# Cross attention's scores: the product of high queries with low keys on half of the array's rows, two query tiles side by side

## The chip, the cores and the metric

The kernel runs on one core of a Trainium2 chip. The metric is the device time of one execution in microseconds. The core's engines work side by side, each with its own queue, and meet by semaphores: TensorE (PE in the rows; PEld is its loading of weights), VectorE (DVE), ScalarE (ACT), GpSimd (POOL), and SyncE (SP), which here issues the loads and stores.

## The reference, cut to what matters

One decoder block over 4 batches of 512 rows by 512 columns, in float32: self attention with 16 heads, cross attention with 8 heads of 64 without projections, and a feed-forward with ternary weights, each behind a layer norm and added to its input. The change is in cross attention:

```
qh = q.reshape(B, h, dq, Lq);  kh = k.reshape(B, h, dq, Lk);  vh = v.reshape(B, h, dv, Lk)
scale = 1.0 / jnp.sqrt(jnp.asarray(dq, dtype=q.dtype))
qk = jnp.einsum('bhdq,bhdl->bhql', qh, kh) * scale
sm = jax.nn.softmax(qk, axis=-1)
ret = jnp.einsum('bhql,bhdl->bhdq', sm, vh)
...
x = x + _L0_xattn_ref(_layernorm(x, axis=-1), ctx_2048, ctx_2048, L0_xattn_gamma)
```

Here B = 4, h = 8, dq = dv = 64 and Lq = Lk = 512: a head's scores are a 512x512 matrix with a contraction over 64.

## The kernel before

Two parts follow each other on the one core. Self attention runs first, in two passes of two batches. Then comes the part that the change touches, in five turns (`turns`): turn 0 is cross attention of batch 0 alone; turns 1, 2 and 3 are cross attention of batch b with the feed-forward of batch b-1 woven between; the last turn is the feed-forward of batch 3 alone. Turns 1 and 2 are two rounds of one loop. In the trace, turn 0 begins at 812 us, turn 1 at 901, turn 2 at 1015, turn 3 at 1133.

Products are made in a reduced float32 format (`F32R`). So that they come out precise, an operand is split in a high part, a rounded copy, and a low part, which is what the copy lost. A query head has only 64 rows, so the array's 128 rows hold both parts at once: `qst` has the query's high part on rows 0 to 63 and its low part on rows 64 to 127, and `kh` and `kl` hold the key's high and low part on both halves. One product of 128 rows by 512 columns with `kh` gives (high + low query) x high key, a second one with `kl` adds (high + low query) x low key. Two products per tile of 128 queries make the scores in one bank of PSUM (lines 394 and 395, in `pe_sx`).

A turn walks 8 heads, and a head 4 query tiles; such a step is called a slot here. In a slot of head h and tile q every engine does its piece, in an order that is written out by hand:

- TensorE (`pe_turn`): scores of tile q (`pe_sx`); in slot 0 four transposes for the values (`pe_vt`, L372); four transposes of the probabilities of tile q of the head before (`pe_pt`, L384); in slots 1 and 3 half of an earlier head's output (`pe_ret`, L406 and L407, 8 products of 256 columns); and, in 22 of the 32 slots of turns 1 to 3, one piece of the feed-forward (`pe_up`, L420 and L421, 8 products of 512 columns).
- VectorE (`dve_turn`): the maximum of the score tile (L595), the low part of the values (slot 0, L584), the feed-forward's elementwise work, the low part of the probabilities (L590), the reciprocal, and in slot 0 the next head's queries (`dve_q`, L578).
- ScalarE (`act_turn`): the feed-forward's tanh (L519), the high part of the values (slot 0, L500) and of the probabilities (L505), the exponential of the score tile with its row sum (L509, two instructions: the activation and the read-out of the sum), in slot 0 the preparation of the next head's high parts (`act_prep`, L493 for `kh`, L495 for `qst`), and the high part of the feed-forward's gate (L526).
- POOL (`pool_turn`): normalising the probabilities (L744), the low parts of the next head (`pool_prep`, L734 for `kl`, L738 for `qst`), the low part of the gate (L751).

The score tiles alternate between two banks: tile q goes to bank q mod 2. So the scores of tile q wait until the exponential of tile q-2 has read its bank (`s_free`, in `pe_sx`); the first tile of a head also waits for POOL's low parts (`ql`, `kl`). SyncE loads a head's queries and keys two heads ahead, when POOL and TensorE have read the slot.

Of the kernel before, what the change touches and what calls it, by code (L numbers as in the profile page):

```python
# [16 lines left out]
F32 = mybir.dt.float32  # L17
F32R = mybir.dt.float32r
I32 = mybir.dt.int32
ACT = mybir.ActivationFunctionType  # L20
ALU = mybir.AluOpType
AX = mybir.AxisListType.X

P = 128
B, T, C = 4, 512, 512
# [8 lines left out]
XH, XD = 8, 64  # L34
# [44 lines left out]
def decoder_block(nc, x, ctx, wa, wb, wq_t, bq_col, bkv, bo, gamma, w1t, w3t, w2t, out):  # L79
# [8 lines left out]
    with stack:  # L88
# [3 lines left out]
        s = {}  # L92
# [138 lines left out]
        def sb(name, shape, dt=F32):  # L231
            return mem_b.enter_context(nc.sbuf_tensor(name, shape, dt))
# [10 lines left out]
        x1d = sb("x1d", [P, 2, C])  # L243
        kd = sb("kd", [P, 2, C])
        qst = sb("qst", [P, 2, C], F32R)
        kh, kl = sb("kh", [P, 2, C], F32R), sb("kl", [P, 2, C], F32R)
        vts = sb("vts", [P, 4, CK, P], F32R)
        pe_x = sb("pe_x", [P, 4, C])
# [7 lines left out]
        s_bank, t_bank, r_bank, u_bank = bank[0:2], bank[2:4], bank[4], bank[5:7]  # L256
        y_bank = [bank[7], bank[5]]

        S_TILES = 4 * XH
# [14 lines left out]
        def pieces(n):  # L274

            if n < 0 or n >= S_TILES:
                return range(0)
            return range(U_PIECES * n // S_TILES, U_PIECES * (n + 1) // S_TILES)
# [88 lines left out]
        def pe_vt(pe, b, h):  # L367
            pe.wait_ge(s[f"kd_in{h % 2}"], b * 128 + 32 * (h // 2 + 1))
            pe_wait(pe, "t_free", t_v(b, h), 2)
            tb = t_bank[(5 * h - 4 if h else 0) % 2]  # L370
            for c in range(CK):
                mm = pe.transpose(tb[:, c * P:(c + 1) * P], kd[:, h % 2, c * P:(c + 1) * P], ident[:])  # L372
            mm.then_inc(s["t_ready"], 1)

        def pe_wait(pe, free, index, ring):
            if not isinstance(index, int) or index >= ring:
                pe.wait_ge(s[free], index - (ring - 1))

        def pe_pt(pe, b, h, q):
            pe.wait_ge(s["xpn"], b * S_TILES + (4 * h + q + 1))  # L380
            pe_wait(pe, "t_free", t_p(b, h, q), 2)
            tb = t_bank[t_p(0, h, q) % 2]
            for c in range(CK):
                mm = pe.transpose(tb[:, c * P:(c + 1) * P], pe_x[:, q, c * P:(c + 1) * P], ident[:])  # L384
            mm.then_inc(s["t_ready"], 1)

        def pe_sx(pe, b, h, q):
            if q == 0:
                pe.wait_ge(s["ql"], b * XH + (h + 1))
                pe.wait_ge(s["kl"], b * XH + (h + 1))  # L390
            pe_wait(pe, "s_free", b * S_TILES + (4 * h + q), 2)
            lhs = qst[:, h % 2, q * P:(q + 1) * P]

            pe.matmul(s_bank[q % 2][:], lhs, kh[:, h % 2, :], start=True, stop=False)  # L394
            pe.matmul(s_bank[q % 2][:], lhs, kl[:, h % 2, :], start=False, stop=True).then_inc(s["s_ready"], 1)  # L395

        def pe_ret(pe, b, h, half):

            n = b * XH + h
            pe.wait_ge(s["t_free"], t_p(b, h, 2 * half + 1) + 1)  # L400
            if half == 0:
                pe_wait(pe, "r_free", n, 1)
            cols = slice(2 * P * half, 2 * P * (half + 1))
            for c in range(CK):
                lhs = vts[:, h % 4, c, :]
                pe.matmul(r_bank[:, cols], lhs, pxh[:, c, cols], start=c == 0, stop=False)  # L406
                mm = pe.matmul(r_bank[:, cols], lhs, pxl[:, c, cols], start=False, stop=c == CK - 1)  # L407
            mm.then_inc(s["r_ready"], 1)

        def pe_up(pe, f, piece):  # L410
            i, w = piece // 2, piece % 2
            m = chunk_rows(i)
            if piece == 0:
                pe.wait_ge(s["w_in"], 64)
                pe.wait_ge(s["t_free"], t_x3(f, TJ))
                pe.wait_ge(s["y"], 1 + f * TJ)
            pe.wait_ge(s[f"u{w}_free"], 1 + f * HC + i)
            for c in range(CK):
                lhs = w13[:, w, c, i * P:i * P + m]
                pe.matmul(u_bank[w][0:m, :], lhs, x3h[:, c, :], start=c == 0, stop=False)  # L420
                mm = pe.matmul(u_bank[w][0:m, :], lhs, x3l[:, c, :], start=False, stop=c == CK - 1)  # L421
            mm.then_inc(s[f"u{w}_ready"], 1)

        def pe_down(pe, f, t):
            pe.wait_ge(s["gl2"], 1 + f * HC + HC)
            if t >= 2:
                pe.wait_ge(s["y"], 1 + f * TJ + (t - 1))
            if t == 1:
                pe.wait_ge(s["u0_free"], 1 + f * HC + HC)
            for i in range(HC):  # L430
                k = chunk_rows(i)
                pe.matmul(y_bank[t % 2][:], gth[0:k, i, t * P:(t + 1) * P], w2[0:k, i, :], start=i == 0, stop=False)  # L432
                mm = pe.matmul(y_bank[t % 2][:], gtl[0:k, i, t * P:(t + 1) * P], w2[0:k, i, :], start=False, stop=i == HC - 1)  # L433
            mm.then_inc(s["y_ready"], 1)

        def pe_x3(pe, b, t):
            pe.wait_ge(s["x3n"], b * TJ + (t + 1))
            pe_wait(pe, "t_free", t_x3(b, t), 2)
            tb = t_bank[t_x3(0, t) % 2]
            for c in range(CK):  # L440
                mm = pe.transpose(tb[:, c * P:(c + 1) * P], pe_x[:, t, c * P:(c + 1) * P], ident[:])
            mm.then_inc(s["t_ready"], 1)

        def pe_turn(pe, b, f, nxt):
            for h in range(XH):
                for q in range(4):
                    if b is not None:
                        pe_sx(pe, b, h, q)
                        if q == 0:
                            pe_vt(pe, b, h)  # L450
                        if h:
                            pe_pt(pe, b, h - 1, q)
                        if q == 1 and h >= 2:
                            pe_ret(pe, b, h - 2, 1)
                        if q == 3 and h >= 1:
                            pe_ret(pe, b, h - 1, 0)
                    if f is not None:
                        for piece in pieces(4 * h + q):
                            pe_up(pe, f, piece)
            if b is not None:  # L460
                pe_pt(pe, b, XH - 1, 0)
                pe_ret(pe, b, XH - 2, 1)
                pe_pt(pe, b, XH - 1, 1)
                pe_pt(pe, b, XH - 1, 2)
            if f is not None:
                pe_down(pe, f, 0)
            if b is not None:
                pe_pt(pe, b, XH - 1, 3)
                pe_ret(pe, b, XH - 1, 0)
                pe_ret(pe, b, XH - 1, 1)  # L470
            if f is not None:
                for t in range(1, TJ - 1):
                    pe_down(pe, f, t)
            if b is not None:
                pe_x3(pe, b, 0)
                pe_x3(pe, b, 1)
            if f is not None:
                pe_down(pe, f, TJ - 1)
            if b is not None:
                for t in range(2, TJ):  # L480
                    pe_x3(pe, b, t)

        def stage_b_pe(pe):
            turns(pe.Fori, lambda b, f, nxt: pe_turn(pe, b, f, nxt))


        def act_prep(act, b, h):

            n, slot = b * XH + h, h % 2
            act.wait_ge(s[f"kd_in{slot}"], b * 128 + 32 * (h // 2 + 1))  # L490
            if h >= 2 or not isinstance(b, int) or b > 0:
                act.wait_ge(s["s_ready"], b * S_TILES + 4 * (h - 1))
            act.activation(kh[:, slot, :], kd[:, slot, :], ACT.Copy).then_inc(s["kh"], 1)  # L493
            act.wait_ge(s["xq"], n + 1)
            act.activation(qst[:, slot, :], x1d[:, slot, :], ACT.Copy).then_inc(s["qh"], 1)  # L495

        def act_vt(act, b, h):
            tb = t_bank[(5 * h - 4 if h else 0) % 2][:].rearrange("p (c n) -> p c n", n=P)
# [232 lines left out]
        def pool_prep(pool, b, h):  # L731
            n, slot = b * XH + h, h % 2
            pool.wait_ge(s["kh"], n + 1)
            pool.tensor_tensor(kl[:, slot, :], kd[:, slot, :], kh[:, slot, :].bitcast(F32), ALU.subtract).then_inc(s["kl"], 1)  # L734
            pool.wait_ge(s["qh"], n + 1)

            pool.wait_ge(s["kl"], n + 1)
            pool.tensor_tensor(qst[XD:P, slot, :], x1d[XD:P, slot, :], qst[XD:P, slot, :].bitcast(F32), ALU.subtract).then_inc(s["ql"], 1)  # L738
            pool.wait_ge(s["ql"], n + 1)

        def pool_prob(pool, b, h, q):
# [776 lines left out]
```

## Time and profile before

| | |
|---|---|
| time, median of 3 runs | 1315.93 us (1315.62 to 1319.83) |
| the profiled execution, first to last instruction | 1316.8 us |
| TensorE busy | 1175.0 us, 89% |
| VectorE busy | 817.9 us, 62% |
| POOL busy | 620.2 us, 47% |
| ScalarE busy | 570.6 us, 43% |
| mean granted TensorE clock | 0.968 |

The profiled execution's own time is its span of 1316.8 us. Busy time is what an engine spends in instructions; consecutive instructions of one engine overlap, so the distance between two starts tells more of the rate than a duration does. In the timelines a row is: start in us from the span's start, duration in us, engine, line, operation, what is written and read, its shape, how many were merged in the row, and in brackets the idle time of the engine before it and what ended it.

### The profile page before, as it was taken

What the parts mean: (1) busy time and instruction counts of PE and PEld (TensorE: products, weight loads), DVE (VectorE), ACT (ScalarE), POOL (GpSimd) and SP (SyncE); (2) the same over time, 40 slices, a digit from 0 to 9 for tenths busy, and PEclk for the clock granted to TensorE, in tenths of its full rate; (3) what the DMA queues carried; (4) which work ended last, traced back from release to release, by engine and by line L of the source; (5) the groups of instructions that cost most, each with busy time, mean ns of one, the idle gap of its engine ahead of it and who ended that gap; (6) DMA issues with size and microseconds to landing.
All of it is one profiled execution on the core that took longest, in us unless ns stands there. A gap on an engine that the chain in (4) does not pass through costs nothing.

```text
span 1316.8 us, 18217 instructions
## 1 busy us (share of the span) xinstructions
PE 1175.0 (89%) x5728; PEld 955.6 (73%) x5728; DVE 817.9 (62%) x1430; ACT 570.6 (43%) x1193; POOL 620.2 (47%) x516
## 2 busy tenths in 40 slices
PE   3859989999995799988999997777999999999998
PEld 2648867777774578876777785566887787888786
DVE  8645665433448576666564657887885787688531
ACT  5323343424335224343323322766762874577130
POOL 3156764535433336764525442654651664365031
PEclk9889999999998799999999998998999999999999
DMA  6232242044152024242425413382111211210000
GB/s 223 73 128 80 80 142 73 26 127 135 40 168 80 0 78 139 80 137 80 150 93 172 135 64 112 97 302 72 47 47 44 85 32 40 89 49 17 33 1 32
DMA packets 52594, 118.56 MB, mean 90 GB/s; under 512 B 11413, under 2 KB 11413, under 8 KB 50482
## 3 DMA queue, kind: packets, MB, share of 16 engines
q1 hardware_dynamic: 52530, 117.79, 27.6%
q8 instruction: 30, 0.49, 0.2%
q14 instruction: 34, 0.28, 0.1%
HBM read 100.96 MB, written 16.81 MB: 89 GB/s over the span
## 4 chain that ended last, share of the span: by engine, by line
PE 49%; DVE 18%; issue 12%; POOL 10%; ACT 7%; DMA 3%; SPq 0%; POOLq 0%; DVEq 0%; ACTq 0%
POOL work L1438 7%; PE bank L74 7%; PE bank L76 6%; PE bank L75 6%; PE bank L421 6%; PE bank L420 6%; DVE raw_a L1257 5%; PE bank L384 4%; PE bank L432 3%; PE bank L433 3%; POOL wal L1432 3%; PE bank L394 2%; PE bank L395 2%; PE bank L406 2%; PE bank L407 2%
## 5 line engine op out<-in xcount | busy, mean ns | idle before, releaser
L1438 POOL TENSOR_TENSOR work<-tmp,work 128x512 fp32r<-128x512 f32 x120 | 154.2, 1295 | 247.8 <-ACT work L1134 163.6
L744 POOL TENSOR_SCALAR pe_x<-pe_x,xri,gam 128x512 f32<-128x512 f32 x128 | 101.0, 790 | 107.0 <-DVE xri L599 101.2
L420 PE MATMUL bank<-x3h,w 128*128 128x512 f32 (+1 forms) x352 | 141.4, 402 | 1.6 <-DVE x3l L664 1.6
L421 PE MATMUL bank<-x3l,w 128*128 128x512 f32 (+1 forms) x352 | 139.1, 395 | 0.0
L1432 POOL TENSOR_TENSOR wbl<-raw_b,wbh 128x512 fp32r<-128x512 f32 x64 | 91.2, 1459 | 64.1 <-ACT wbh L1082 64.1
L74 PE MATMUL bank<-wah,xth 128*128 128x512 f32 x256 | 101.7, 397 | 15.4 <-POOL wal L1432 15.4
L1432 POOL TENSOR_TENSOR wal<-raw_a,wah 128x512 fp32r<-128x512 f32 x64 | 92.3, 1472 | 47.6 <-ACT wah L1089 47.6
L74 PE MATMUL bank<-wbh,gh 128*128 128x512 f32 x256 | 103.1, 403 | 13.0 <-DVEq L1306 11.7
L74 PE MATMUL bank<-wbh,work 128*128 128x512 f32 x256 | 102.3, 399 | 6.9 <-DVE work L1323 4.9
L509 ACT ACTIVATE pe_x<-bank,xmx 128x512 f32<-128x512 f32 x128 | 87.8, 686 | 40.6 <-DVE xmx L595 39.3
L595 DVE TENSOR_REDUCE xmx<-bank 128x1 f32<-128x512 f32 x128 | 87.4, 683 | 27.3 <-PE bank L395 24.1
L1323 DVE TENSOR_TENSOR work<-bank,work 128x512 fp32r<-128x512 f32 x64 | 44.2, 691 | 96.6 <-ACT work L1140 96.3
L1317 DVE TENSOR_TENSOR tmp<-bank,bkv_bc 128x512 f32<-128x512 f32 x64 | 44.2, 691 | 92.8 <-PE bank L76 47.5
L76 PE MATMUL bank<-wbh,gl 128*128 128x512 f32 x256 | 101.8, 398 | 0.0
L75 PE MATMUL bank<-wbl,gh 128*128 128x512 f32 x256 | 101.8, 398 | 0.0
L75 PE MATMUL bank<-wal,xth 128*128 128x512 f32 x256 | 100.8, 394 | 0.0
L76 PE MATMUL bank<-wah,xtl 128*128 128x512 f32 x256 | 100.8, 394 | 0.0
L76 PE MATMUL bank<-wbh,work 128*128 128x512 f32 x256 | 100.0, 391 | 0.0
L1134 ACT ACTIVATE work<-tmp 128x512 fp32r<-128x512 f32 x64 | 40.4, 631 | 137.4 <-DVE tmp L1317 137.4
L75 PE MATMUL bank<-wbl,work 128*128 128x512 f32 x256 | 99.9, 390 | 0.0
L590 DVE TENSOR_TENSOR pxl<-bank,pxh 128x512 fp32r<-128x512 f32 x128 | 87.5, 686 | 14.4 <-ACT pxh L505 13.7
L1276 DVE SCALAR_TENSOR_TENSOR tmp<-bkv_bc,shat,bank 128x512 f32<-128x512 f32 x64 | 47.8, 746 | 78.0 <-POOL work L1438 44.3
(158 smaller groups left out, 3063.6 us busy)
## 6 DMA issues: line engine op xcount, KB each, us to landing
raw_b<-in_wb SPq DMA_DIRECT2D x16, 1024.0 KB, 5.6
raw_a<-in_wa SPq DMA_DIRECT2D x16, 1024.0 KB, 5.4
x1d<-x_scratch SPq DMA_DIRECT2D x64, 128.0 KB, 2.7
kd<-in_ctx SPq DMA_DIRECT2D x64, 128.0 KB, 2.7
ternary_scratch<-wraw SPq DMA_DIRECT2D x12, 682.5 KB, 5.6
wraw<-in_w1t SPq DMA_DIRECT2D x8, 682.5 KB, 4.9
wraw<-in_w3t SPq DMA_DIRECT2D x8, 682.5 KB, 7.2
wraw<-in_w2t SPq DMA_DIRECT2D x8, 682.5 KB, 9.5
```

Source lines behind the costliest of these rows:

```text
L74: pe.matmul(out, wh, xh, start=start, stop=False)
L75: pe.matmul(out, wh, xl, start=False, stop=False)
L76: return pe.matmul(out, wl, xh, start=False, stop=stop)
L420: pe.matmul(u_bank[w][0:m, :], lhs, x3h[:, c, :], start=c == 0, stop=False)
L421: mm = pe.matmul(u_bank[w][0:m, :], lhs, x3l[:, c, :], start=False, stop=c == CK - 1)
L509: act.activation(pe_x[:, q, :], s_bank[q % 2][:], ACT.Exp, bias=xmx[:, q:q + 1], accum_out=xrs[:, q:q + 1]).then_inc(s["s_free"], 1)
L590: dve.tensor_tensor(pxl[:, :, q * P:(q + 1) * P], tb, pxh[:, :, q * P:(q + 1) * P].bitcast(F32), ALU.subtract).then_inc(s["t_free"], 1)
L595: dve.reduce_max(xmx[:, q:q + 1], s_bank[q % 2][:], axis=AX, negate=True).then_inc(s["xmx"], 1)
L744: pool.tensor_scalar(pe_x[:, q, :], pe_x[:, q, :], xri[:, q:q + 1], gam[:], ALU.mult, ALU.mult).then_inc(s["xpn"], 1)
L1257: dve.tensor_tensor(raw_a[:, c, :], raw_a[:, c, :], beta_bc[:], ALU.add).then_inc(s["beta_add"], 1)
L1432: pool.tensor_tensor(low[:, c, :], raw[:, c, :], high[:, c, :].bitcast(F32), ALU.subtract).then_inc(s[f"w{which}l"], 1)
L1438: pool.tensor_tensor(low, tmp[:, slot, :], high.bitcast(F32), ALU.subtract).then_inc(s["mvl"], 1)
```

## The change

Per pair of query tiles the two products with `kh` stay as they are. The two products with `kl` are cut to the high query: for the first tile they use rows 0 to 63 of `qst` and `kl`, for the second rows 64 to 127 of a new tile `qsd`, which holds the high query on its upper half, and of `kl`. The two halves of the array work on different tiles and banks. What is left out is low query x low key.

- TensorE: `pe_sx` is called for q = 0 and 2 only, and makes the scores of q and q + 1: wait for bank q, product with `kh`; wait for bank q + 1, product with `kh`; then the two half products, each of which reports its tile as ready.
- ScalarE: the copy of `qst` covers rows 0 to 63; a second copy writes the high query to rows 64 to 127 of `qsd`. Each counts up `qh`.
- POOL: waits for two counts of `qh` per head, and takes the low query on rows 64 to 127 from `qsd` instead of from the same rows of `qst`.

```diff
+        qsd = sb("qsd", [P, 2, C], F32R)
...
         def pe_sx(pe, b, h, q):
             if q == 0:
                 pe.wait_ge(s["ql"], b * XH + (h + 1))
                 pe.wait_ge(s["kl"], b * XH + (h + 1))
-            pe_wait(pe, "s_free", b * S_TILES + (4 * h + q), 2)
-            lhs = qst[:, h % 2, q * P:(q + 1) * P]
-
-            pe.matmul(s_bank[q % 2][:], lhs, kh[:, h % 2, :], start=True, stop=False)
-            pe.matmul(s_bank[q % 2][:], lhs, kl[:, h % 2, :], start=False, stop=True).then_inc(s["s_ready"], 1)
+            for r in (q, q + 1):
+                pe_wait(pe, "s_free", b * S_TILES + (4 * h + r), 2)
+                pe.matmul(s_bank[r % 2][:], qst[:, h % 2, r * P:(r + 1) * P], kh[:, h % 2, :], start=True, stop=False)
+            for r, of, part in ((q, qst, slice(0, XD)), (q + 1, qsd, slice(XD, P))):
+                pe.matmul(s_bank[r % 2][:], of[part, h % 2, r * P:(r + 1) * P], kl[part, h % 2, :], start=False, stop=True).then_inc(s["s_ready"], 1)
...
-                        pe_sx(pe, b, h, q)
+                        if q % 2 == 0:
+                            pe_sx(pe, b, h, q)
...
-            act.activation(qst[:, slot, :], x1d[:, slot, :], ACT.Copy).then_inc(s["qh"], 1)
+            act.activation(qst[0:XD, slot, :], x1d[0:XD, slot, :], ACT.Copy).then_inc(s["qh"], 1)
+            act.activation(qsd[XD:P, slot, :], x1d[XD:P, slot, :], ACT.Copy).then_inc(s["qh"], 1)
...
-            pool.wait_ge(s["qh"], n + 1)
+            pool.wait_ge(s["qh"], n * 2 + 2)
...
-            pool.tensor_tensor(qst[XD:P, slot, :], x1d[XD:P, slot, :], qst[XD:P, slot, :].bitcast(F32), ALU.subtract).then_inc(s["ql"], 1)
+            pool.tensor_tensor(qst[XD:P, slot, :], x1d[XD:P, slot, :], qsd[XD:P, slot, :].bitcast(F32), ALU.subtract).then_inc(s["ql"], 1)
```

## Rows read from the trace of the kernel before

**Rows 1.** Busy time by stretch: length, then per engine, clock, DMA share, GB/s.
```profile
847.60:865.02 17.42, 13.92 (x88) 10.85 (x89) 15.66 (x34) 13.01 (x31) 11.41 (x12) 1.00 0.42 130
1036.03:1092.47 56.44, 56.38 (x333) 47.94 (x332) 47.84 (x96) 40.86 (x89) 36.71 (x37) 1.00 0.17 47
```
**Rows 2.** Groups by line: busy us, mean ns, idle before them and its releasers.
```profile
L394 PE MATMUL bank<-kh,qst 128*128 128x512 f32 x128 | 56.3, 440 | 15.6 <-ACT pe_x L509 15.5
L495 ACT ACTIVATE qst<-x1d 128x512 fp32r<-128x512 f32 x32 | 20.1, 630 | 10.2 <-DVE x1d L578 9.2
```
**Rows 3.** Timeline of TensorE, turn 2, head 6.
```profile
1080.92 0.40 PE L394 MATMUL bank<-kh,qst 128*128 128x512 f32 x1
1081.16 0.40 PE L395 MATMUL bank<-kl,qst 128*128 128x512 f32 x1
1081.39 0.60 PE L372 MATMUL bank<-ident,kd 128*128 128x128 f32 x4
1081.83 0.60 PE L384 MATMUL bank<-ident,pe_x 128*128 128x128 f32 x4
...
1085.99 0.40 PE L394 MATMUL bank<-kh,qst 128*128 128x512 f32 x1
...
1086.81 0.48 PE L420 MATMUL bank<-x3h,w 128*128 128x512 f32 x1
1087.13 0.40 PE L421 MATMUL bank<-x3l,w 128*128 128x512 f32 x1
...
1088.76 0.40 PE L394 MATMUL bank<-kh,qst 128*128 128x512 f32 x1
```
**Rows 4.** Timeline of ScalarE in that head, and busy time of its last stretch.
```profile
1084.68 0.63 ACT L495 ACTIVATE qst<-x1d 128x512 fp32r<-128x512 f32 x1 [0.42 <-DVE x1d L578]
1085.22 0.61 ACT L526 ACTIVATE gth<-gf 128x512 fp32r<-128x512 f32 x1
...
1087.35 0.21 ACT L509 ACTIVATION_READ_ACCUMULATOR pe_x<-bank,xmx 128x1 f32 x1
...
1084.68:1087.56 2.88, 2.88 (x22) 2.65 (x21) 2.28 (x4) 2.88 (x7) 2.73 (x3) 1.00 0.20 3
```
**Rows 5.** Timelines, turn 2, heads 2 to 4: tile 2's scores, exp(1)'s read-out.
```profile
1041.07 0.40 PE L394 MATMUL bank<-kh,qst 128*128 128x512 f32 x1
1041.39 0.20 ACT L509 ACTIVATION_READ_ACCUMULATOR pe_x<-bank,xmx 128x1 f32 x1
...
1052.87 0.39 PE L394 MATMUL bank<-kh,qst 128*128 128x512 f32 x1
1053.42 0.20 ACT L509 ACTIVATION_READ_ACCUMULATOR pe_x<-bank,xmx 128x1 f32 x1
...
1064.64 0.40 PE L394 MATMUL bank<-kh,qst 128*128 128x512 f32 x1
1064.80 0.19 ACT L509 ACTIVATION_READ_ACCUMULATOR pe_x<-bank,xmx 128x1 f32 x1
```
**Rows 6.** Timelines, head 0 of turns 2 and 3: tile 2's scores and a read-out.
```profile
1020.59 0.19 ACT L509 ACTIVATION_READ_ACCUMULATOR pe_x<-bank,xmx 128x1 f32 x1
1020.84 0.50 PE L394 MATMUL bank<-kh,qst 128*128 128x512 f32 x1 [1.33 <-ACT pe_x L509]
...
1136.74 0.39 PE L394 MATMUL bank<-kh,qst 128*128 128x512 f32 x1
1137.86 0.20 ACT L509 ACTIVATION_READ_ACCUMULATOR pe_x<-bank,xmx 128x1 f32 x1
```
**Rows 7.** Timelines of three engines, turn 0, head 6, and the turn's end.
```profile
866.07 0.19 ACT L509 ACTIVATION_READ_ACCUMULATOR pe_x<-bank,xmx 128x1 f32 x1
866.24 0.63 PE L384 MATMUL bank<-ident,pe_x 128*128 128x128 f32 x4
...
869.92 0.69 DVE L590 TENSOR_TENSOR pxl<-bank,pxh 128x512 fp32r<-128x512 f32 x1
...
887.99 0.55 DVE L578 TENSOR_SCALAR x1d<-x1d,stx 128x512 f32<-128x512 f32 x1 [0.98 <-DMA x1d<-x_scratch]
```

## The prediction

> **What bounds the kernel now.** I read the busy table by stretch first, then the groups by line, then three timelines: TensorE and ScalarE over one head of the third turn, the same two instructions in other heads, and one head of the first turn. (A turn is one batch of cross attention, with the feed-forward of the batch before beside it; a head has four slots, one per query tile.)
>
> The table [rows 1] shows two regimes. In turn 2, heads 2 to 6, TensorE is busy 56.38 of 56.44 us at the full granted clock (1.00, the 2.4 GHz level), VectorE 47.84, ScalarE 40.86: TensorE is the bound, the others have slack but not much. In turn 0, where no feed-forward runs, TensorE is busy 13.92 of 17.42 us and VectorE 15.66: there a loop of waits between the engines is the bound. The groups by line [rows 2] say what TensorE waits for ahead of the first score product: 15.6 us in all, for the exponential (L509), which frees the score bank.
>
> So TensorE's work counts in 48 of the 64 pairs of query tiles (turns 1 to 3), but only as long as it doesn't wait. The edit saves a little of it and moves a wait.
>
> **Part 1, the products.** A score tile is two full products now, started 0.24 us (1080.92, 1081.16) and 0.23 us apart; I use 0.235 [rows 3]. A pair of tiles costs 4 x 0.235 = 0.94 us. After: two full products (0.47) and one step L in which two half-array products run side by side. No row of before shows half the rows in use, so L is bounded. Below: one step, 0.235, with perfect overlap. Above: the halves in series, 0.47, with the array running empty on both sides; a product lasts 0.40 and its follower starts after 0.235 [rows 3], so 0.165 each side, 0.80 in all. The nearest row is a change of kind that the trace does show: the first product behind a group of transposes takes 0.32 (1086.81 to 1087.13) instead of 0.235 [rows 3]. I take L = 0.32. A pair then saves 0.94 - 0.79 = 0.15 us (0.145 before rounding), 48 pairs 7.0 us; with the bounds, from +11 us saved to -16 us.
>
> Rows show no price for switching to part of the array. The Trainium skill, "TensorEngine Tiling (Array Packing)", Key Properties, says that a change of tiling mode drains TensorE, which speaks against this change: every pair switches in and out. Its page "TensorE: Matmul & The Clock Gate", Measured speedup vs the span model, speaks for it: tiles start about 4 ns apart, which as an estimate puts L at 0.24 us without a drain. No row here shows either; the drain is a rival below.
>
> **Part 2, the wait that moves.** A bank pair alternates, so tile q needs the exponential of tile q-2. Now slot 3 waits for exp(1). After the change both products of tiles 2 and 3 stand at the head of slot 2, so TensorE waits for exp(1) one slot earlier, and behind that wait are queued tile 2's and 3's low products, the transposes of the last head's probabilities and the feed-forward products of slot 2. In turn 2 head 6 that is the work between 1085.99 and 1088.76, 2.77 us [rows 3]. In the same way tile 1 waits for exp(3) of the head before, in slot 0.
>
> Is exp(1) done by then? In head 6 its read-out ends at 1087.35 + 0.21 = 1087.56 [rows 4], while slot 2 starts at 1085.99 [rows 3]: 1.57 us late. Today this costs nothing, as only slot 3 (1088.76) needs it. Three things move it. (a) The pair stands ahead of slot 0's transposes (1081.39 [rows 3]): 0.79 instead of 0.465, so they and all that hangs on them (the value split, the probability split, the exponential of tile 0) come 0.325 later. (b) ScalarE gets a second 64x512 copy per head, between `qst` and exp(1). Its cost goes by free size: the copy of 128x512 takes 630 ns [rows 2] and the next instruction starts 0.54 after it (1084.68, 1085.22) [rows 4]; a cost by partitions would be half that, the other bound; I take 0.54, since the elements per partition are unchanged. From `qst` to the end of exp(1) ScalarE has no pause in head 6 (the row by stretch [rows 4]), so it lies on the path. (c) From the end of a read-out to the product that waited for it there is 0.06 (1020.59 + 0.19 to 1020.84 [rows 6]). TensorE reaches tile 3's first product at: start of slot 2 now, minus slot 1's scores (0.465), plus 0.325, plus tile 2's first product (0.235), so 0.095 later than slot 2 starts now. The wait is therefore: lateness now + 0.325 + 0.54 + 0.06 - 0.095 = lateness + 0.83.
>
> Lateness in turn 2 [rows 5]: head 2, 1041.59 against 1041.07, 0.52; head 3, 1053.62 against 1052.87, 0.75; head 4, 1064.99 against 1064.64, 0.35; head 6, 1.57. Waits: 1.35, 1.58, 1.18, 2.40, together 6.5 us a turn. In heads 5 and 7 exp(1) is done before slot 2 begins, and head 7 has no next head to prepare: nothing. Head 0, from turn 3: 1138.06 against 1136.74, 1.32 late [rows 6], wait 2.1; in turn 2 TensorE already idles 1.33 us there [rows 6], so I count it in two turns only. Head 1 I take like head 2, 1.3. Sum: 3 x 6.5 + 2 x 2.1 + 3 x 1.3 = 27.6 us. After each of these 17 waits the first product takes 0.32 for 0.235 (taken from the step after transposes): 1.4 us. Turns 1 to 3: 27.6 + 1.4 - 7.0 = +22.0 us.
>
> What is late next? exp(3) of such a head: tile 3 is now scored at the front of slot 2, a slot earlier, and two slots of TensorE work follow before the next head's tile 1 asks for it. I count nothing there; if that cover fails (a head with feed-forward in one of these slots only) some 0.5 us more in a head.
>
> **Part 3, turn 0.** No feed-forward covers anything here. In head 6 tile 0 starts now as soon as exp(2) is done; after, both low products also need exp(3) of head 5, whose read-out ends at 866.07 + 0.19 = 866.26 [rows 7]. Then 0.06, a product of 0.32, L = 0.32: the value transposes start at 866.96, and 0.44 behind them (1081.39 to 1081.83 [rows 3]) those of the probabilities, at 867.40 instead of 866.24 [rows 7]: 1.16 late. The chain behind it, probability split, VectorE, the `qst` copy, has no cover, so behind the second copy the probability split of tile 1 comes 1.16 + 0.54 = 1.7 later, and with it VectorE's half of it at 869.92 [rows 7]; VectorE then goes through the rest of the head in order. Heads without the statistics step on VectorE lose less; I take 1.5 for heads 2 to 6 and half of it for 1 and 7: 9.0 us. VectorE idles 0.98 us for a landing at the turn's end (887.99) [rows 7], which hides that much: +8.0 us.
>
> **At no cost.** POOL's subtraction for `qst` now waits for two copies; between stands its own `kl` subtraction, longer than the added copy, and TensorE needs the result three slots later. SyncE's loads wait for the same counts as before. If POOL's cover is gone, the added copy's 0.54 would be late by that much, again under three slots of slack. The dropped product of the two low parts changes no time but L's own.
>
> **Sum.** 22.0 + 8.0 = +30 us on the profiled execution's 1316.8 us span, which is 0.9 above the median of 1315.93; I add it to the median: 1346.
>
> **The rivals.**
> 1. *TensorE is the bound and the waits are hidden*: 48 x 0.145 = 7.0 us up to 48 x 0.235 = 11.3 us gained, 1305 to 1309, and at most 64 x 0.235 = 15 us, 1301. The mechanism: the score of tile 1 is ready a slot earlier, VectorE's maximum and the exponential follow earlier, so exp(1) is done when slot 2 starts. For it: rows 1, where TensorE has no idle time. Against it: in head 6 exp(1) follows ScalarE's own queue, not the score [rows 4], and that queue gets longer. It decides if the waits add to under 7 us, a quarter of my sum.
> 2. *The halves don't run side by side, or each switch drains the array.* L is then 0.47 + 0.085, or 0.235 + 2 x 0.165, both about 0.56, 0.24 above mine. The waits stay (both sides move together); 48 pairs cost 11.5 us more, and the 8 pairs in turn 0 that head a chain 2 us: 1360. Both together (L = 0.80): 1374. In the series case the change doesn't do what it says. The drain is the page's rule; no row speaks for or against it beyond the 0.085 after transposes.
> 3. *The two balance*: waits of about a third of my sum (9 us) against a saving of 9 to 11 us, with turn 0 unmoved: 1312 to 1320. It needs ScalarE's chain to have slack that rows 4 don't show.
>
> **How the numbers follow.** Forecast (waits at the head of the slot, halves side by side, 1322 to 1356): 0.60. Rival 2 (1355 to 1374): 0.18. Rival 1 (1301 to 1311): 0.14. Rival 3: 0.08. A measurement of this kernel can tell about 0.3% (4 us) from no change. Slower by more: 0.60 + 0.18 = 0.78; same: 0.08; faster: 0.14. The range from 1314 to 1364 leaves out rival 1 and the upper part of rival 2, about 0.2; the forecast's own range is 1322 to 1356.
>
> **What would show it.** Right: idle time ahead of L394's products grows from 15.6 us to some 40 or more, released by the exponential, and lies in turns 1 to 3 as well; the wait in turn 2 head 6 is over 2 us and head 5 has none; TensorE's busy time in those heads falls under 95% of the stretch; a 64x512 copy of 0.6 us stands twice per head on ScalarE; the two half products start within 0.05 us. Rival 2: half products starting 0.2 us apart, or steps over 0.3 us on both sides. Rival 1: TensorE gap-free as now and each head some 0.3 us shorter. I would be wrong above all if exp(1) ended earlier than its old chain says, since three quarters of the loss hang on it.

## The result and the profile after

The changed kernel takes 1389.88 us (median of 4 runs, 1386.32 to 1390.62) against 1316.08 us for the kernel before beside it: ratio 1.0553, 95% interval 1.0533 to 1.0573. It is 74 us slower where 30 were forecast (1346), and above the range's upper end of 1364. The sign came as forecast, and so did the place and roughly the length of the waits; the size of the loss did not.

First the page of the changed kernel: its span, TensorE's row (busy time, share, instructions) and the granted clock in 40 slices, in tenths.

```profile
span 1388.8 us, 18265 instructions
...
PE 1203.3 (87%) x5728; PEld 954.4 (69%) x5728; DVE 821.0 (59%) x1430; ACT 595.5 (43%) x1225; POOL 620.9 (45%) x516
...
PEclk9989989999998999999999968989999999999999
```

Then its groups by line (busy us, mean ns | idle before them and what ended it). The first answers to the L394 row of [rows 2], and the two copies to its L495 row.

```profile
L396 PE MATMUL bank<-kh,qst 128*128 128x512 f32 x128 | 54.6, 463 | 56.1 <-ACT pe_x L514 55.9
...
L398 PE MATMUL bank<-kl,qst 64*128 64x512 f32 x64 | 33.9, 530 | 0.0
...
L398 PE MATMUL bank<-kl,qsd 64*128 64x512 f32 x64 | 33.8, 529 | 0.0
...
L499 ACT ACTIVATE qst<-x1d 64x512 fp32r<-64x512 f32 x32 | 20.1, 628 | 10.2 <-DVE x1d L583 9.2
...
L500 ACT ACTIVATE qsd<-x1d 64x512 fp32r<-64x512 f32 x32 | 20.1, 629 | 0.8
```

The reader sees TensorE's idle time ahead of the first score product grow from 15.6 us to 56.1, released by the exponential, and a copy of half the partitions cost what the whole copy cost (0.63 us).

Next the busy time by stretch (length, then PE, PEld, DVE, ACT, POOL, granted clock, DMA share, GB/s): turns 0, 1 and 2, and turn 2's heads 2 to 6, which answers to the second of [rows 1].

```profile
809.40:919.70 110.30, 71.04 (x369) 51.30 (x368) 76.46 (x179) 60.38 (x131) 45.45 (x48) 0.81 0.41 134
919.70:1051.00 131.30, 119.15 (x635) 92.71 (x633) 87.99 (x183) 74.96 (x159) 59.46 (x59) 0.97 0.17 47
1051.00:1185.00 134.00, 119.66 (x635) 92.67 (x633) 87.88 (x184) 75.24 (x159) 59.49 (x59) 0.96 0.16 47
1076.51:1144.06 67.55, 60.32 (x333) 46.80 (x332) 48.40 (x97) 44.75 (x94) 37.81 (x39) 0.97 0.14 39
```

The same five heads take 67.55 us instead of 56.44. TensorE is busy 89% of them instead of all, and its busy time itself grew by 3.9 us, at a mean clock of 0.97 instead of 1.00.

Last the place that the prediction was worked out on: turn 2, head 6, TensorE and then ScalarE, to be laid beside [rows 3] and [rows 4].

```profile
1134.73 0.39 PE L396 MATMUL bank<-kh,qst 128*128 128x512 f32 x1
...
1137.61 0.50 PE L396 MATMUL bank<-kh,qst 128*128 128x512 f32 x1 [2.49 <-ACT pe_x L514]
1138.05 0.50 PE L398 MATMUL bank<-kl,qst 64*128 64x512 f32 x1
1138.05 0.50 PE L398 MATMUL bank<-kl,qsd 64*128 64x512 f32 x1
1138.48 0.66 PE L385 MATMUL bank<-ident,pe_x 128*128 128x128 f32 x4
```

```profile
1134.54 0.63 ACT L500 ACTIVATE qsd<-x1d 64x512 fp32r<-64x512 f32 x1
1135.20 0.63 ACT L531 ACTIVATE gth<-gf 128x512 fp32r<-128x512 f32 x1
...
1136.30 0.59 ACT L510 ACTIVATE pxh<-bank 128x512 fp32r<-128x512 f32 x1
1136.78 0.69 ACT L514 ACTIVATE pe_x<-bank,xmx 128x512 f32<-128x512 f32 x1
1137.35 0.21 ACT L514 ACTIVATION_READ_ACCUMULATOR pe_x<-bank,xmx 128x1 f32 x1
```

Tile 2's product starts at 1134.73; tile 3's stands behind it and waits until exp(1) is read out at 1137.56, while the copy of L500 lies on ScalarE's unbroken chain to it. The two halves start together and last 0.50 each. This is the forecast's picture.

The loss by turn, from the first score product of a turn to that of the next (one profiled execution of each kernel; the starts of before are 812.4, 900.5, 1015.3 and 1132.7). The rows below the first two are the kernels of the next section; the score tiles alternate between two banks where nothing else is said:

| | turn 0 | turn 1 | turn 2 | turn 3 to the end |
|---|---|---|---|---|
| before | 88.1 | 114.8 | 117.4 | 184.1 |
| changed | 110.3 | 131.3 | 134.0 | 203.8 |
| pair order alone | 102.0 | 122.3 | 125.7 | 192.7 |
| pair order and second copy | 109.8 | 129.1 | 130.4 | 200.4 |
| second copy alone | 95.7 | 117.7 | 120.8 | 188.5 |
| before, three banks | 88.2 | 115.0 | 116.9 | 185.6 |
| pair order, three banks | 89.6 | 116.6 | 118.3 | 186.7 |
| pair order and second copy, three banks | 96.2 | 119.2 | 120.9 | 189.8 |
| changed, three banks | 96.2 | 120.3 | 122.9 | 190.7 |

Turn 0 alone lost 22.2 us (forecast 8.0), the rest 52.8 (forecast 22.0).

### The profile page after: what moved, and what is told of

Same layout as the page of the kernel before. It is cut to its first block, busy times and chain, and to the rows that moved or that the text cites. A ratio compares the mean times of both kernels' runs of the same rounds, so it can differ in the third digit from the quotient of the medians.

```text
span 1388.8 us, 18265 instructions
## 1 busy us (share of the span) xinstructions
PE 1203.3 (87%) x5728; PEld 954.4 (69%) x5728; DVE 821.0 (59%) x1430; ACT 595.5 (43%) x1225; POOL 620.9 (45%) x516
## 4 chain that ended last, share of the span: by engine, by line
PE 44%; DVE 19%; issue 13%; ACT 10%; POOL 10%; DMA 2%; POOLq 0%; SPq 0%; DVEq 0%; ACTq 0%
POOL work L1443 6%; PE bank L74 6%; PE bank L76 6%; PE bank L75 6%; DVE raw_a L1262 5%; PE bank L423 5%; PE bank L424 5%; PE bank L435 3%; PE bank L436 3%; PE bank L385 3%; POOL wal L1437 3%; PE bank L396 2%; PE bank L398 2%; ACT pe_x L514 2%; ACT pxh L510 2%
## 5 line engine op out<-in xcount | busy, mean ns | idle before, releaser
L423 PE MATMUL bank<-x3h,w 128*128 128x512 f32 (+1 forms) x352 | 146.7, 417 | 1.7 <-DVE x3l L669 1.6
L424 PE MATMUL bank<-x3l,w 128*128 128x512 f32 (+1 forms) x352 | 143.8, 409 | 0.0
L74 PE MATMUL bank<-wbh,gh 128*128 128x512 f32 x256 | 103.0, 402 | 13.5 <-DVEq L1311 11.9
L510 ACT ACTIVATE pxh<-bank 128x512 fp32r<-128x512 f32 x128 | 75.9, 596 | 74.4 <-PE bank L385 72.6
L396 PE MATMUL bank<-kh,qst 128*128 128x512 f32 x128 | 54.6, 463 | 56.1 <-ACT pe_x L514 55.9
```

The lines of the kernel that those rows point to most:

```text
L74: pe.matmul(out, wh, xh, start=start, stop=False)
L396: pe.matmul(s_bank[r % 2][:], qst[:, h % 2, r * P:(r + 1) * P], kh[:, h % 2, :], start=True, stop=False)
L510: act.activation(pxh[:, :, q * P:(q + 1) * P], tb, ACT.Copy).then_inc(s["pxh"], 1)
```

## The experiments

**The order, the copy and the halves, one by one.** The change has three parts: the pair of tiles scored together, the second copy, and the half-array products. Two kernels take parts away from it, two add one to the kernel before.

The order and the copy, with full low products:

```diff
-            for r, of, part in ((q, qst, slice(0, XD)), (q + 1, qsd, slice(XD, P))):
-                pe.matmul(s_bank[r % 2][:], of[part, h % 2, r * P:(r + 1) * P], kl[part, h % 2, :], ...)
+            for r in (q, q + 1):
+                pe.matmul(s_bank[r % 2][:], qst[:, h % 2, r * P:(r + 1) * P], kl[:, h % 2, :], ...)
```

> The change with its half products made full again (128 rows of qst against kl for both tiles): the order in pairs and ScalarE's second copy stay, the array never switches. Theory (the wait moved to the head of slots 0 and 2, its idle times halving TensorE's clock, and the second copy before it make most of the loss; the switch of the array is a smaller part): 1360 to 1380 us, idle time ahead of the first score products near the 56 us of the change, a pair of tiles without a wait 0.94 us. Rival (the switch to half the array and back makes most of it): under 1340 us.

The order alone, that is the same edit and the one copy as before (POOL as before, too):

```diff
-            act.activation(qst[0:XD, slot, :], x1d[0:XD, slot, :], ACT.Copy).then_inc(s["qh"], 1)
-            act.activation(qsd[XD:P, slot, :], x1d[XD:P, slot, :], ACT.Copy).then_inc(s["qh"], 1)
+            act.activation(qst[:, slot, :], x1d[:, slot, :], ACT.Copy).then_inc(s["qh"], 1)
```

> The order in pairs alone: as e1, and ScalarE makes the high query in one copy as before. Theory: 1345 to 1365 us, each of the waits in heads 2, 3, 4 and 6 about 0.6 to 0.8 us shorter than in the change (0.54 for the copy, the rest for the shorter pair). Rival (the order costs nothing by itself, the copy makes the wait late): within 8 us of before, 1308 to 1324. Rival (the switch): the same.

The second copy alone, in the kernel before (the diff of the copies the other way round, and POOL subtracts from `qsd`):

> The kernel before with ScalarE's second 64x512 copy alone, in slots and products of before (the low query is taken from the second copy, so it is used). Theory: covered in turns 1 to 3, where slot 3 asks for exp(1) 1.2 us or more after it ends, and about 0.5 us a head in turn 0: 1316 to 1322 us. Rival (the copy makes the loss): over 1335 us.

The half product alone, in the kernel before, tile by tile in its old slot:

```diff
-            pe.matmul(s_bank[q % 2][:], lhs, kl[:, h % 2, :], start=False, stop=True)
+            pe.matmul(s_bank[q % 2][:], qst[0:XD, h % 2, q * P:(q + 1) * P], kl[0:XD, h % 2, :], start=False, stop=True)
```

> The kernel before with the low product of every tile cut to rows 0 to 63, in before's slots and without the second copy: 128 half products, none beside another (low query x low key is left out, as in the change). Theory: each tile then takes 0.33 + 0.43 us from its full product to what follows instead of 2 x 0.235, as the trace of the change shows around a half product, so +0.29 us for each of 96 tiles in turns 1 to 3, 28 us, and some 5 us in turn 0: 1340 to 1355 us, with TensorE free of waits for the exponential in turns 1 to 3. Rival (a half product costs no more than a full one, and what the change shows around it comes from the two side by side): 1311 to 1321 us.

Measured, all beside the same runs of the kernel before: order and copy 1378.15 us, ratio 1.0439 (1.0420 to 1.0457); order alone 1352.07, 1.0245 (1.0220 to 1.0271); copy alone 1332.5, 1.0090 (1.0069 to 1.0110); half products alone 1350.53, 1.0248 (1.0220 to 1.0276). The order with the copy, the order alone and the half products came as expected; the copy alone cost more than its theory allowed (1316 to 1322). The idle time ahead of the first score product in the groups by line, for the order with the copy, the order alone, the copy alone and the half products alone:

```profile
L396 PE MATMUL bank<-kh,qst 128*128 128x512 f32 x128 | 54.3, 458 | 56.6 <-ACT pe_x L514 56.2
```
```profile
L396 PE MATMUL bank<-kh,qst 128*128 128x512 f32 x128 | 53.4, 453 | 39.6 <-ACT pe_x L513 37.3 <-DVE pxl L594 1.9
```
```profile
L395 PE MATMUL bank<-kh,qst 128*128 128x512 f32 x128 | 57.8, 452 | 19.9 <-ACT pe_x L511 19.9
```
```profile
L394 PE MATMUL bank<-kh,qst 128*128 128x512 f32 x128 | 56.9, 445 | 9.4 <-ACT pe_x L509 9.4
```

Of the 56.1 us of waiting, 15.6 were there before; the order alone has 39.6, 24 more, and the copy brings the rest. The copy without the order costs 13 us too: in turn 0, where [rows 1] show no cover, the stretch grows from 88.1 to 95.7 us and its granted clock is 0.80, against 0.91 before (before, then with the copy):

```profile
812.40:900.50 88.10, 62.22 (x369) 48.01 (x368) 75.50 (x179) 53.68 (x123) 45.38 (x48) 0.91 0.51 169
```
```profile
810.30:906.00 95.70, 70.14 (x370) 56.29 (x368) 76.52 (x179) 60.06 (x131) 45.46 (x48) 0.80 0.47 154
```

The half product has half the rows and still costs time, though TensorE waits less than before (9.4 us). Its timeline (turn 2) tells why: the half product starts 0.32 us behind the full one, and the next instruction 0.43 behind the half product, where [rows 3] have 0.24 and 0.23.

```profile
1062.56 0.40 PE L394 MATMUL bank<-kh,qst 128*128 128x512 f32 x1
1062.88 0.49 PE L395 MATMUL bank<-kl,qst 64*128 64x512 f32 x1
1063.31 0.66 PE L372 MATMUL bank<-ident,kd 128*128 128x128 f32 x4
```

**Do the halves run side by side?** The changed kernel with both half products on the same rows, so that they can only run one after the other, and one copy:

```diff
-            for r, of, part in ((q, qst, slice(0, XD)), (q + 1, qsd, slice(XD, P))):
-                pe.matmul(s_bank[r % 2][:], of[part, h % 2, r * P:(r + 1) * P], kl[part, h % 2, :], ...)
+            for r in (q, q + 1):
+                pe.matmul(s_bank[r % 2][:], qst[0:XD, h % 2, r * P:(r + 1) * P], kl[0:XD, h % 2, :], ...)
```

> The change with both half products of a pair on rows 0 to 63, so one behind the other, and with ScalarE's one copy as before (the second tile needs no high query on the upper half then): order and switch of the change, no copy, nothing side by side. Theory (side by side the second half product is free, 0.235 us a pair; the copy makes the waits longer and costs 24 to 27 us inside the change, as between e1 and e2): the pair takes 0.235 + 0.33 + 0.235 + 0.43 us, 64 x 0.235 = 15 us more less what waits hide, and 24 to 27 us less for the copy: 1373 to 1382. Rival 1 (both halves share the array in time anyway, or the second costs a switch of its own): pair times as in the change, or over 1.4 us. Rival 2 (the copy costs little inside the change): 1390 or more.

1381.02 us, ratio 1.0460 (1.0434 to 1.0486), as expected. A pair in the changed kernel and one here, both without a wait ahead of it:

```profile
1144.06 0.62 PE L396 MATMUL bank<-kh,qst 128*128 128x512 f32 x2
1144.61 0.50 PE L398 MATMUL bank<-kl,qst 64*128 64x512 f32 x1
1144.62 0.50 PE L398 MATMUL bank<-kl,qsd 64*128 64x512 f32 x1
1145.04 0.66 PE L373 MATMUL bank<-ident,kd 128*128 128x128 f32 x4
```
```profile
1139.58 0.63 PE L396 MATMUL bank<-kh,qst 128*128 128x512 f32 x2
1140.14 0.73 PE L398 MATMUL bank<-kl,qst 64*128 64x512 f32 x2
1140.80 0.66 PE L373 MATMUL bank<-ident,kd 128*128 128x128 f32 x4
```

Side by side the pair takes 0.98 us, in series 1.22: the second half costs 0.24 there and nothing in the changed kernel. So the halves do run side by side. But 0.98 is more than the 0.94 of four full products, since the switch takes 0.09 on the way in (0.327 for 0.235) and 0.195 on the way out (0.43 for 0.235), 0.285 together, and the second half saves 0.235. The whole kernel is nevertheless 9 us faster than the changed one. It has one copy, and it lost less to the clock (below); the two were not separated here.

**Take the wait away.** A third score bank (bank 7, which is free while a turn's scores are made) lets tile q wait for exp(q-3) instead of exp(q-2):

```diff
-        s_bank, t_bank, r_bank, u_bank = bank[0:2], bank[2:4], bank[4], bank[5:7]
+        s_bank, t_bank, r_bank, u_bank = [bank[0], bank[1], bank[7]], bank[2:4], bank[4], bank[5:7]
...
-                pe_wait(pe, "s_free", b * S_TILES + (4 * h + r), 2)
-                pe.matmul(s_bank[r % 2][:], ...)
+                s_wait(pe, b, 4 * h + r)
+                pe.matmul(s_bank[(4 * h + r) % 3][:], ...)
```

In the changed kernel:

> The change with a third bank for scores (bank 7, which the feed-forward's last product uses only when a turn's scores are done): tile q then waits for exp(q-3), so the pair in slot 2 needs exp(0) instead of exp(1). All else of the change stays. Theory (the wait in slots 0 and 2 makes most of the loss, with the clock behind it): no idle time ahead of the score products in turns 1 to 3, full granted clock there, and 1310 to 1330 us: 48 pairs cost 0.05 us more each by the switch, the rest is turn 0. Rival (switch or copy make the loss): over 1360 us.

In the kernel before:

> The kernel before with the same third bank, to set e5 beside. Theory: turns 1 to 3 unchanged, since TensorE has no idle time there; turn 0, where the score products wait some 14 us for exponentials, gains 2 to 8 us: 1308 to 1315 us. Rival (turn 0 is bound by VectorE's queue, and the wait for the bank only passes that on): 1314 to 1318 us.

With the order alone:

> The order in pairs alone (full products, one copy) with the third bank: against e2 it takes away the wait and nothing else. Theory (the order's 33 us are the wait): 1316 to 1326 us, with no idle time ahead of the score products in turns 1 to 3. Rival (the order costs by what it puts in front of the transposes and VectorE's work, not by the wait): over 1335 us.

With the order and the second copy, full products:

> The change's order, its second copy and a third score bank, but with full-height low products: the kernel of e5 without the half-array switch, or that of e8 with the second copy. It splits the 25 us that the change still costs over before with three banks (1.9%). If the copy is what is left of it, as its cost alone in before says (+12 to 13.6 us), and the switch costs 0.05 us a pair (48 pairs, 2.4 us, and a few in the first turn), it takes 1335 to 1342 (copy 13 to 17 us over the kernel with three banks and one copy, which was 4.5 over before). If the switch is the larger part, it stays within 1322 to 1330, near the kernel with one copy.

Measured: the changed kernel 1343.8 us, ratio 1.0192 (1.0165 to 1.0218), which misses both expectations; before 1318.16, 0.9989 (0.9978 to 1.0000), no difference to tell, so its theory (a gain of 2 to 8 us) missed and its rival, a turn 0 bound elsewhere, came nearest (1314 to 1318); the order 1322.44, 1.0034 (1.0016 to 1.0052); the order and the copy 1337.72, 1.0148 (1.0123 to 1.0172), both as expected, but that the order alone still waits 2.2 us in turn 2. The idle time ahead of the first score product, in the same sequence:

```profile
L406 PE MATMUL bank<-kh,qst 128*128 128x512 f32 x128 | 46.3, 433 | 8.5 <-ACT pe_x L524 5.4 <-POOL qst L753 3.1
```
```profile
L404 PE MATMUL bank<-kh,qst 128*128 128x512 f32 x128 | 56.1, 439 | 4.5 <-POOL qst L748 4.5
```
```profile
L406 PE MATMUL bank<-kh,qst 128*128 128x512 f32 x128 | 44.8, 419 | 7.1 <-ACT pe_x L523 4.1 <-POOL qst L752 2.9
```
```profile
L406 PE MATMUL bank<-kh,qst 128*128 128x512 f32 x128 | 46.0, 432 | 8.8 <-ACT pe_x L524 5.4 <-POOL qst L753 3.4
```

The wait of the kernel before (15.6 us) was worth nothing: 12.9 us of it lie in turn 0, and that turn takes 88.2 us without it, 88.1 with it. The wait of the changed kernel was worth 3.6% (1.0553 to 1.0192), some 47 us. The order, which costs 32 us with two banks, costs 4 with three. With most of the waits gone the parts can be read one by one: order 0.34%, copy 1.14% (15 us), halves 0.44% (6 us; the intervals of the last two kernels overlap a little, and in the turns of their profiles they lie 4.0 us apart). Of the copy's 15 us, 6.6 fall in turn 0, where the granted clock is 0.92 without it and 0.85 with it (the order alone, then with the copy):

```profile
809.90:899.50 89.60, 61.11 (x370) 48.55 (x368) 75.91 (x179) 53.84 (x123) 45.39 (x48) 0.92 0.50 166
```
```profile
807.90:904.10 96.20, 65.25 (x369) 52.99 (x368) 76.22 (x179) 60.08 (x131) 45.41 (x48) 0.85 0.47 154
```

**The clock behind the waits.** Turn 1's head 6 in the changed kernel is longer than the same head of turn 2, and turn 2's head 2 longer than the same head of turn 1 (13.51 us); in both the clock is below 1:

```profile
993.94:1010.01 16.07, 13.58 (x70) 10.65 (x68) 10.26 (x20) 8.85 (x19) 7.90 (x9) 0.89 0.14 35
1129.56:1144.06 14.50, 12.01 (x69) 9.44 (x68) 10.23 (x20) 8.97 (x19) 7.92 (x9) 1.00 0.16 37
1076.50:1091.60 15.10, 13.63 (x69) 10.54 (x68) 9.55 (x20) 9.13 (x19) 8.38 (x9) 0.89 0.12 35
```

TensorE's timeline in that head 2 has the wait, then products that last 0.63 instead of 0.40 and start 0.43 apart, then the old ones again:

```profile
1083.55 0.50 PE L396 MATMUL bank<-kh,qst 128*128 128x512 f32 x1 [1.47 <-ACT pe_x L514]
...
1085.20 0.63 PE L424 MATMUL bank<-x3l,w 128*128 128x512 f32 x1
1085.63 0.63 PE L423 MATMUL bank<-x3h,w 128*128 128x512 f32 x1
...
1090.67 0.39 PE L423 MATMUL bank<-x3h,w 128*128 128x512 f32 x1
1090.90 0.40 PE L424 MATMUL bank<-x3l,w 128*128 128x512 f32 x1
```

To test whether the idle time brings this, products into an unused bank fill the waits of the changed kernel:

```diff
             for r in (q, q + 1):
+                if r == q + 1:
+                    if isinstance(b, int) and b == 0:
...
+                        count = 5 if q == 2 else (4 if h in (1, 3, 6) else 0)
+                    else:
+                        count = (8, 3, 5, 5, 3, 0, 9, 0)[h] if q == 2 else 0
+                    for k in range(count):
+                        pe.matmul(bank[7][:], qst[:, h % 2, q * P:(q + 1) * P], kh[:, h % 2, :], start=True, stop=True)
                 pe_wait(pe, "s_free", b * S_TILES + (4 * h + r), 2)
```

> The change with filler products while TensorE waits: between the first and the second full product of a pair it repeats the first one into bank 7, which nobody reads then, 3 to 9 times in slot 2 of the heads of turns 1 to 3 that wait (at 0.235 us each less than the wait measured there, 0.9 to 2.65 us) and 4 or 5 times in turn 0. The fillers compute nothing that is used. Theory (the idle time halves TensorE's granted clock for 3.4 us at a time, and each such stretch costs some 1.6 us of products that run at half rate): full clock in heads 1 to 7 of turns 1 to 3, heads 2 and 6 of all three turns at 13.5 and 14.5 us as in the change's undisturbed ones, and 8 to 15 us less than the change in all, 1375 to 1382. Rival (the clock falls whatever TensorE does in the wait, or costs nothing there): 1386 to 1392, heads as in the change.

1378.5 us, ratio 1.0459 (1.0426 to 1.0493), as the clock's theory expected: TensorE does 151 products for nothing (52 of them in turn 0), and the kernel is 11 us faster than the changed one. Heads 2 and 6 take 13.5 and 14.5 us in all of turns 1 to 3, as in the changed kernel where its clock is 1.00. Turn 2 has the clock at 1.00 throughout:

```profile
1048.40:1179.30 130.90, 123.69 (x666) 96.18 (x665) 87.85 (x184) 75.02 (x159) 59.42 (x59) 1.00 0.17 49
```

The profile of the filled kernel is 12.2 us shorter: 1.5 in turn 0, 1.7 and 3.1 in turns 1 and 2, 3.1 in turn 3, and 2.8 at the end of the last turn, where nothing was filled (more on this place below).

The full-rate time lost to a low clock in turns 1 to 3 (length times one minus granted clock, summed over stretches of 2 us, from where the low clock that each kernel has at the end of turn 0 is over): before 0, the changed kernel 11.9 us in six stretches, with the filling 0, order and copy 6.8, halves in series 6.8, order alone 1.7, copy alone 1.7, changed with three banks 1.7, order and copy with three banks 0. Such a figure is what the clock can have cost at most, since parts of the stretches lie in waits.

## Why the prediction was right in sign and wrong in size

The wait moved to the head of the slot, as the forecast said. What failed are terms of its sum: L was too small, so that the pairs cost time instead of saving it, the clock behind the waits and the transposes that wait for VectorE stood in it at nothing, and turn 0 was taken at 8 us where it lost 22.

**Part 2, the waits: right, a little low.** The sum of lateness, second copy, start-up and position gave 2.40 us in turn 2's head 6; the trace has 2.49 idle, and 2.65 from the first product to the second beyond the usual 0.235. The other heads by that measure: head 2 1.63 (forecast 1.35), head 3 1.37 (1.58), head 4 0.90 (1.18), head 1 0.9 (1.3), heads 5 and 7 none. Head 0 waits 2.2 to 2.9 in all three turns, where 2.1 was counted in two. Turns 1 to 3 together 32.4 us against 27.6. The exp(3) that "what is late next" put at 0.5 us in a head does show once in turn 2: 0.47 at head 5. Most of the waiting is the order's, as forecast: 39.6 us of idle time with the order alone, 17.0 more with the copy.

**Part 1, the products: the step L was mis-sized, and the second half of rival 2 comes close to what happened.** I took 0.32 for L from the first product behind a group of transposes; the trace has 0.327 to get into the half array and 0.43 to get out, so L, counted as the text counts it, is 0.52 (0.99 a pair less two products of 0.235). The halves do start together, 3 to 4 ns apart; they don't run in series. 48 pairs were to save 7.0 us and cost 48 x 0.05 = 2.4 instead: 9.4 us on the wrong side. The halves with three banks agree: 4.0 us in the turns of the profiles, of which up to 1.7 are the clock. The Trainium skill, "TensorEngine Tiling (Array Packing)", Key Properties, says that changing the tiling mode drains TensorE. This trace agrees in that both switches cost time: a product starts 0.43 us behind a half product and 0.235 behind a full one, and the 0.52 of L is close to the 0.56 of the drain in rival 2; that it is a drain is not shown. I gave that rival 0.18. The 4 ns between tile starts that the Trainium skill gives in "TensorE: Matmul & The Clock Gate", Measured speedup vs the span model, agree with the 3 to 4 ns here.

**The clock: a term that the sum didn't have.** The sum priced a wait at its own length plus 0.085 for the restart. In turns 1 to 3 the granted clock, which never fell there in the profiled execution of the kernel before, went to 0.50, the 1.2 GHz level, in six stretches behind or within such waits, 11.9 us of full-rate time. That the idle time brings this was shown by filling it: no stretch is left there, heads 2 and 6 are 1.55 to 1.6 us shorter each time that the clock had fallen in them (in two of the three turns each), and heads 0 and 1 of turn 2 are 1.4 shorter together, 7.7 us in all. So the clock cost about 8 us in these turns, and 11.9 at most.

**Part 3, turn 0: mechanism found, size off by 14 us.** Heads 2 to 6 lose 2.6 us each (56.37 against 43.15 us), where 1.5 was forecast. Heads 0 and 1 lose 8.9 us together (26.98 against 18.08); I had 0.75 for head 1 and nothing for head 0. There the granted clock is at 0.50 through this whole stretch:

```profile
815.40:835.90 20.50, 11.59 (x35) 7.14 (x36) 11.29 (x39) 8.55 (x20) 7.74 (x8) 0.50 0.39 135
```

Before, it was at half rate up to 814 and from 817 to 824 only. How much of the 8.9 us is the clock was not separated, but it isn't most: with three banks the changed kernel takes 20.4 us for the two heads, at a mean clock that is no better (0.59, with two banks 0.57). In heads 2 to 6 the clock makes some 2 of the 13.2 us: with the filling, which keeps it at 1.00 there, they take 54.3. The third bank takes 14.1 us of turn 0's 22.2 back (96.2 against 110.3), so the waits make most of it; the copy makes 6.6 of the remaining 8.1, by the pair of kernels with three banks.

**"At no cost": half right.** POOL's longer wait and the subtraction from `qsd` delay nothing (55.9 of the 56.1 us of idle time are the exponential's). But in turns 1 to 3 I counted the copy only where its 0.54 us reach a score product, and it costs 15 us where hardly such a wait is left: 6.6 in turn 0, the rest spread over the later turns. It delays the chain of the probabilities on ScalarE and VectorE, as their transposes show with three banks (the order alone, then with the copy): they wait 8.1, then 15.2 us for VectorE's low part of the probabilities.

```profile
L385 PE MATMUL bank<-ident,pe_x 128*128 128x128 f32 x512 | 77.0, 276 | 17.5 <-DVE vts L598 9.4 <-DVE pxl L604 8.1
```
```profile
L385 PE MATMUL bank<-ident,pe_x 128*128 128x128 f32 x512 | 77.7, 276 | 24.9 <-DVE pxl L605 15.2 <-DVE vts L599 9.7
```

In the changed kernel these transposes wait 13.0 us against 5.9 before, but that is the order's doing: the order alone has the same 13.0, most of it for the values' low part (`vts`).

**The sum again.** Behind turn 0 the kernel lost 52.8 us: waits 32.4, and 1.5 ahead of tile 2 in turn 2's head 0, less the 2.7 that before idled there too; pairs 2.4; restarts 1.7 (20 waits more than before at 0.085); transposes waiting for VectorE 4.2; the clock 7.7 to 11.9. That is 47 to 51. Another 2.8 us lie at the end of the last turn. TensorE waits 2.83 us there for the low part of the gate, in both kernels alike; behind this wait the clock falls in the profiled execution of the changed kernel and not in that of before, and from there to the end it takes 26.5 us instead of 23.7. The kernel before with three banks has such a fall at that place too (25.3), so this part may be chance and not the change. With turn 0 (22.2), and 3 us gained ahead of it, in the part that the change doesn't touch, the profiled 72 us are accounted for to within some 3 us. By removal, in this order, the ratio's 5.5% (73 us) are: two banks under this order 47, second copy 15, half products 6, order 4.5.

**The rivals.** Rival 1 (waits hidden) and rival 3 (balance) are out: TensorE is busy 89%, not all, of heads 2 to 6 of turn 2. Rival 2's price for the switch is in, its series is out, and with it alone the forecast would have been 1360, still 30 us short: the larger miss is turn 0 and the clock, which no rival had.

**What stays open.** Why the clock falls behind some waits and not behind others of the same length (head 6 waits 2.49 us in turns 1 and 2, and only in turn 1 the clock falls), and how turn 0's loss, the copy's part of it above all, splits between the chain of waits and the clock. The accounts by turn rest on one profiled execution of each kernel, and the mean granted clock of the kernel before went from 0.963 to 0.973 over its runs. No version here beats the kernel before.

## What to carry to other kernels

Before two tiles are put side by side, ask what the pair will now wait for: with as many buffers as tiles in a pair, both must be free at once, and the wait moves a step forward, in front of all that is queued behind it. The first thing to try is one more buffer; here it gave back 47 of 74 us. Half-height products side by side have to pay for the switch: here one pair saved 0.235 us and the switch to half the array and back took 0.285, so by these numbers several pairs behind one switch would pay, which no run here tried. And a wait that opens on a TensorE that was never idle costs more than its length, since the clock may fall behind it (here some 1.6 us a head where it did); a stage whose clock is 1.00 because it has no gap has that to lose.

## What the runs showed of the hardware

- A change from the full array to half its rows started the next product 0.327 us after the last instead of 0.235, and the change back 0.43 instead of 0.235 (512 columns, full clock). Two products on different halves of the rows started 3 to 4 ns apart and lasted 0.50 each; on the same half the second cost 0.24.
- In turns 1 to 3 of the changed kernel, waits of 1.5 to 2.7 us in a stream of products at 2.4 GHz were followed, in six places, by stretches at 1.2 GHz (granted clock 0.50); other waits of the same lengths were not. One such stretch cost a head 1.57 us (16.07 against 14.50). Products without use in these waits kept the clock at 1.00.
- ScalarE's copy of 64 partitions took 0.628 us, that of 128 took 0.630: half the partitions save nothing.
